# Second mixer of a two-layer recurrent block: score tile, row tile and items slot by slot on TensorE, exits of items per slot on ScalarE and VectorE

## The chip, the cores and the metric

The kernel runs on one core of one Trainium2 chip. The metric is the device time of one execution in microseconds (us). Three runs of the kernel before took 1249.71, 1252.53 and 1256.12 us; the median is 1252.53 us.

## The reference

Two layers over 2048 tokens of width 128. Only the attention of the second layer (the "second mixer") matters here. With 16 heads of size 64:

```
q, k, v = jnp.einsum('bsx,xAnh->Abnsh', input, w)
q = q + q_bias[:, None, :]
a = jnp.einsum('bnqh,bnkh->bnqk', q, k) * h ** (-0.5)
emb = jnp.einsum('sf,fnh->nsh', sins, positional * FREQS ** (-0.5))
pos_scores = jnp.einsum('bnqh,nvh->bnqv', q, emb) * h ** (-0.5)
a = a + relative_causal(pos_scores)
a = jax.nn.softmax(jnp.where(mask, a, NEG_INF), axis=-1)
o = jnp.einsum('bnqk,bnkh->bqnh', a, v).reshape(b, s, n * h)
out = o @ (out_kernel * (fan_in * fan_out) ** (-0.25)) + out_bias
```

`mask` is causal. The positional part is folded into the key and query rows (64 rows of the head, 32 of positions), so that one product of 96 rows gives `a`. The maximum of each row has to be known before the exponentials are taken; it goes into the product as a 97th row.

## The kernel before

The program before the second mixer (the first layer, its experts, the norms) is untouched and takes the first 433 us. `attention1` then walks over 8 pairs of heads (`PAIRS`). Each pair has 80 slots (`SLOTS`), 40 per head. A slot n of a pair has up to four pieces of work on TensorE:

- `score_tile(p, n)` (L1742 to L1744, three matmuls into `S[n % 2]`): scores of 128 keys (block j) against up to 512 queries (chunk c), transposed. Over a head, chunk c has 4(c+1) blocks; the last four of a chunk are diagonal tiles of 512, 384, 256 and 128 columns. ScalarE takes the exponential (`exps`, L1952) into `prob`; GpSimd splits off the low part (`plow`, L1484). Since there are two `S` buffers, `score_tile` n waits for the exponential of slot n - 2 (`s_exp`).
- `row_tile(p, n)` (L1732, one matmul into `A[n % 2]`): scores the other way round, for the row maxima of a later stretch. VectorE reduces them (`row_max`, L2051 or L2054); `row_tile` n waits for the maximum of slot n - 2 (`s_max`). The last pair has none in its last 24 slots.
- `slot_items(p, n)`: what the planner (`plan_items`) has put into that slot, at most one item: "pos", "q" or "k" (three matmuls of 512 columns, L1700 to L1702) or "v" (twelve of 128 columns, L1708 to L1710) of the next pair, "maxima" (L1713), "turn" (four transposes, L1717) and "project" (eight matmuls, L1723). Items write alternately into two buffers `M`. An item waits until the item two before it has been read out of its buffer (`s_free`). The reading out is called its exit here: "q", "k" and "v" are copied on ScalarE first (L1879, L1881, L1886) and then on VectorE (L2012, L2015, L2018), which waits for ScalarE's copy; "pos" and "project" leave by VectorE alone (L2003, L2008), "maxima" and "turn" by ScalarE alone (L1891, L1893).
- `value_tile` for slot n - 6 (`DRAIN`; L1754 to L1757, into `O`), which waits for GpSimd's `plow`.

Each engine's program is written out by hand, and each engine takes its instructions in that order. TensorE goes in steps of two slots: for slots n and n+1 it issues the score tiles of both, then row tile and items of n, row tile and items of n+1, then the two value tiles. ScalarE does the exponential of every slot, the item exits only after an odd slot (those of the two slots together), and then, at slots 8, 12, 20, 32, 48, 52, 60 and 72, `scaled` (four activations, L1966), which divides a finished chunk of `O` by its sums. VectorE does the row maximum of every slot, the item exits after an odd slot, `join_pos` at odd slots from 11 to 33, and `inverted` (L2131), for which `scaled` waits. In a pair other than the last these items stand in even slots: pos in 8, 14 and 16, turn in 10, 54, 62 and 74, q in 18, 22, 26 and 30, k in 20, 24, 28 and 32, v in 42 and 48, project in 58. The others (pos in 11, v in 55 and 63, maxima, project in 13, 65 and 77) stand in odd ones. The last pair has only turns, projects and maxima.

Of the kernel before, what the change touches and what calls it, by code (L numbers as in the profile page):

```python
# [27 lines left out]
PAIRS = HEADS // 2  # L28
# [39 lines left out]
ALL = PAIRS * SLOTS  # L68
# [26 lines left out]
def plan_items(last):  # L95

    items = {n: [] for n in range(SLOTS)}
    items[SCALE + 1].append(("turn", -1, 3))
    items[SCALE + 4].append(("project", -1, 3))
    for n, a in enumerate(A_SLOTS):  # L100
        if last and a[0] == 2:
            continue
        for c in range(NC):
            if a[1] == a_end(c) - 1 and n + 2 < SLOTS:
                items[n + 2].append(("maxima", a[0], c))
    items[1].append(("maxima", 0, 2))

    def put(n, item):

        while items[n]:  # L110
            n += 1
        items[n].append(item)
        return n

    if not last:
        n = DRAIN + 1
        for kind, c in [("pos", c) for c in range(NC)] + [(kind, c) for c in range(NC) for kind in ("q", "k")]:
            n = put(n + 1, (kind, 1, c)) + 1
        assert n <= NB - 4
    for c in range(NC - 1):  # L120
        n = put(NB + sum(TPC * (k + 1) for k in range(c + 1)) + SCALE + 1, ("turn", 0, c))
        put(n + 3, ("project", 0, c))
    if not last:
        n = NB + 2
        for c in range(NC):
            n = put(n, ("v", 1, c)) + 6
        assert n <= V_SLOT + 4
    return items
# [18 lines left out]
def ahead(p):  # L147

    return isinstance(p, int) and p == -1
# [1185 lines left out]
def attention1(nc, dram, keep, out_dram):  # L1335
# [12 lines left out]
    with ExitStack() as ctx:  # L1348
# [88 lines left out]
        plan = {}  # L1437
        for last in (False, True):
            items, k = plan_items(last), 0
# [21 lines left out]
        def count(tok, p):  # L1461

            n, b, before = tok
            return n + 1 + PER * p, b, before + (PER // 2) * p
# [221 lines left out]
        def _(pe):  # L1686
# [162 lines left out]
            for n in range(0, ALL + DRAIN, 2):  # L1849
                two = (n, n + 1)  # L1850
                for k in two:
                    if k < ALL:
                        score_tile(*divmod(k, SLOTS))
                for k in two:
                    if k < ALL:
                        row_tile(*divmod(k, SLOTS))
                        slot_items(*divmod(k, SLOTS))
                for k in two:
                    if k >= DRAIN:
                        value_tile(*divmod(k - DRAIN, SLOTS))  # L1860
# [6 lines left out]
        def _(act):  # L1867
            def item(kind, rel, c, tok, p, highs):
                it = max(p, 0) if isinstance(p, int) else p
                done, b, _ = count(tok, it)  # L1870
                a0, a1 = c * CW, (c + 1) * CW
                if kind in ("pos", "project"):
                    return
                act.wait_ge(s_item, done)
                if kind in ("q", "k"):
                    if not ahead(p) and kind == "q":
                        act.wait_ge(s_move[c], 2 * MOVES * (p + 1))
                    if kind == "q":
                        act.activation(stage[QHI][:, a0:a1], M[b][:], ACT.Identity, bias=bq[:, p + 1:p + 2]).then_inc(s_high, 1)  # L1879
                    else:  # L1880
                        act.activation(stage[KHI][:, a0:a1], M[b][:], ACT.Copy).then_inc(s_high, 1)  # L1881
                elif kind == "v":
                    if not ahead(p) and c == 0:
                        for h in (0, 1):
                            act.wait_ge(s_mv[h], 16 * (p + 1))
                    act.activation(stage_v[:, TPC * c:TPC * (c + 1), :, 0:HS],  # L1886
                                   M[b][:].rearrange("p (n h d) -> p n h d", n=TPC, h=2), ACT.Copy).then_inc(s_high, 1)
                elif kind == "maxima":
                    if rel > 0:
                        act.wait_ge(s_mrow[c], 16 * (2 * p + rel))  # L1890
                    act.activation(mrow[:, c, :], M[b][0:TPC, 0:P], ACT.Copy, scale=1.0 / M_UNIT).then_inc(s_free[b], 1)  # L1891
                elif kind == "turn":
                    act.activation(oT[:], M[b][:], ACT.Copy).then_inc(s_free[b], 1)  # L1893
# [77 lines left out]
            for n in range(ALL + SCALE):  # L1971
                if n < ALL:
                    exps(*divmod(n, SLOTS))
                    p, at = divmod(n, SLOTS)
                    if at % 2:
                        for (kind, rel, c, tok) in plan[p == PAIRS - 1][at - 1] + plan[p == PAIRS - 1][at]:
                            item(kind, rel, c, tok, p, 0)
                if n == ALL:
                    act.wait_ge(s_gate, NC)
                    for c in range(NC):  # L1980
                        at = gate[:, TPC * c:TPC * (c + 1), :]
                        act.activation(at, at, ACT.Silu).then_inc(s_silu, 1)
                if n >= SCALE:
                    scaled(*divmod(n - SCALE, SLOTS))
            kind, rel, c, tok = fin_items[0]
# [5 lines left out]
        def _(dve):  # L1991
            def item(kind, rel, c, tok, p, high):

                it = max(p, 0) if isinstance(p, int) else p
                done, b, _ = count(tok, it)
                a0, a1 = c * CW, (c + 1) * CW
                if kind in ("maxima", "turn"):
                    return
                dve.wait_ge(s_item, done)
                if kind == "pos":  # L2000
                    if not ahead(p):
                        dve.wait_ge(s_plow, NC * p + c + 1)
                    ins = dve.scalar_tensor_tensor(turned[:, c, :], M[b][:], bpos[:, p + 1:p + 2], angle[:, a0:a1], ALU.add, ALU.mult)  # L2003
                elif kind == "project":
                    if p == 0 and rel < 0:
                        dve.wait_ge(s_bias, 16)
                    s = acc[:, TPC * c:TPC * (c + 1), :]
                    ins = dve.tensor_tensor(s, M[b][:].rearrange("p (n d) -> p n d", d=D), s, ALU.add)  # L2008
                else:
                    dve.wait_ge(s_high, HIGHS * (p + 1) + high + 1)  # L2010
                    if kind == "q":
                        ins = dve.scalar_tensor_tensor(stage[QLO][:, a0:a1], M[b][:], bq[:, p + 1:p + 2], stage[QHI][:, a0:a1],  # L2012
                                                       ALU.add, ALU.subtract)
                    elif kind == "k":
                        ins = dve.tensor_tensor(stage[KLO][:, a0:a1], M[b][:], stage[KHI][:, a0:a1], ALU.subtract)  # L2015
                    elif kind == "v":
                        t = slice(TPC * c, TPC * (c + 1))
                        ins = dve.tensor_tensor(stage_v[:, t, :, HS + 1:VW], M[b][:].rearrange("p (n h d) -> p n h d", n=TPC, h=2),  # L2018
                                                stage_v[:, t, :, 0:HS], ALU.subtract)
                ins.then_inc(s_free[b], 1)  # L2020
# [103 lines left out]
            high = highs[0]  # L2124
# [8 lines left out]
            for n in range(ALL + DRAIN + 2):  # L2133
                if n < ALL:
                    p, at = divmod(n, SLOTS)
                    last = p == PAIRS - 1
                    rel, a = A_SLOTS[at]
                    if not (last and rel == 2):
                        row_max(rel % 2, a, PRO_A + at, p, 2 * p + rel)
                    high = high if at else 0  # L2140
                    if at % 2:
                        for (kind, rel, c, tok) in plan[last][at - 1] + plan[last][at]:
                            item(kind, rel, c, tok, p, high)
                            high += kind in ("q", "k", "v")
                    if at >= JOIN_SLOT and (at - JOIN_SLOT) % 2 == 0 and (at - JOIN_SLOT) // 2 < len(JOINS) and not last:
                        join_pos(*JOINS[(at - JOIN_SLOT) // 2], p)
                if n >= DRAIN + 2:
                    inverted(*divmod(n - DRAIN - 2, SLOTS))
            for c in range(NC):
                s = acc[:, TPC * c:TPC * (c + 1), :].rearrange("p n d -> p (n d)")  # L2150
                if c == NC - 1:

                    tok = fin_items[1][3]
                    dve.wait_ge(s_item, tok[0] + 1)
                    dve.tensor_tensor(s, M[tok[1]][:], s, ALU.add).then_inc(s_free[tok[1]], 1)
                else:
                    tok = next(x[3] for n in range(SLOTS) for x in plan[True][n] if x[:3] == ("project", 0, c))
                    tok = (tok[0], tok[1], count(tok, PAIRS - 1)[2])
# [148 lines left out]
```

## Time and profile before

| what | us |
|---|---|
| profiled execution, its own time | 1252.04 |
| span of its trace | 1250.0 |
| median of three runs | 1252.53 |
| PE busy (matmul) | 1168.7 (93%) |
| POOL busy | 813.2 (65%) |
| DVE busy | 803.7 (64%) |
| ACT busy | 673.5 (54%) |

PE is TensorE's matmuls, PEld its weight loads, DVE is VectorE, ACT ScalarE, POOL GpSimd. The profiled execution's own time is 2.0 us longer than its span. A matmul's row shows its start and a length that includes its way through the array, so the rows of successive matmuls overlap; what a matmul costs its successor is read from start to start.

### The profile page before, as it was taken

How to read it: one execution, taken by the hardware profiler on the slowest of the kernel's cores; microseconds unless marked ns; L12 is line 12 of the kernel's file. 1: busy time of each engine (PE TensorE's matmuls, PEld its weight loads, DVE VectorE, ACT ScalarE, POOL GpSimd, SP SyncE). 2: the span in 40 equal slices, each digit the busy share in tenths (PEclk: the TensorE clock that was granted, in tenths of full speed). 3: DMA queues.
4: the chain of work that ended last, by engine and by line, in shares of the span. 5: the costliest groups of instructions: out<-in, count | busy, mean ns of one | idle time of the engine just before them, and what ended most of it. 6: DMA issues, size and time to landing. Idle time of an engine off the chain costs nothing.

```text
span 1250.0 us, 31158 instructions
## 1 busy us (share of the span) xinstructions
PE 1168.7 (93%) x11813; PEld 759.7 (61%) x11820; DVE 803.7 (64%) x2017; ACT 673.5 (54%) x1375; POOL 813.2 (65%) x1097
## 2 busy tenths in 40 slices
PE   4899679999996999999999999999999999999997
PEld 2354455567772656666665666666666666566665
DVE  3787355752576687577668668757767766865552
ACT  2543142235533556656656656656665665665665
POOL 0777300031434488787787888878778778788886
PEclk9998768999996999999999999999999999999999
DMA  8200200001303322031030230213203113022001
GB/s 320 107 1 1 76 1 1 1 22 56 100 11 77 81 60 44 19 78 28 18 86 10 44 75 21 45 24 72 44 19 74 21 30 85 11 44 62 18 2 35
DMA packets 74752, 60.09 MB, mean 48 GB/s; under 512 B 38950, under 2 KB 69162, under 8 KB 73516
## 3 DMA queue, kind: packets, MB, share of 16 engines
q1 hardware_dynamic: 73580, 56.02, 18.1%
q0 software_dynamic: 1024, 2.09, 0.5%
q8 instruction: 94, 1.54, 0.5%
q14 instruction: 54, 0.44, 0.1%
HBM read 19.70 MB, written 4.72 MB: 20 GB/s over the span
## 4 chain that ended last, share of the span: by engine, by line
PE 63%; ACT 3%; DVE 2%; issue 1%; DMA 0%; DVEq 0%; ACTq 0%
PE S L1742 9%; PE S L1743 9%; PE A L1732 9%; PE S L1744 9%; PE O L1756 5%; PE O L1757 5%; PE O L1754 5%; PE M L1723 2%; PE M L1700 2%; PE M L1701 2%; PE M L1702 2%; ACT prob L1952 1%; ACT otok L1966 1%; PE M L1717 1%; PE M L1708 1%
## 5 line engine op out<-in xcount | busy, mean ns | idle before, releaser
L1484 POOL TENSOR_TENSOR plow<-prob 128x512 f16<-128x512 f32 (+3 forms) x640 | 577.2, 915 | 108.8 <-ACT prob L1952 86.3
L1952 ACT ACTIVATE prob<-S,keep_sigma 128x512 f32<-128x512 f32 (+3 forms) x640 | 384.6, 625 | 270.2 <-PE S L1744 269.7
L2054 DVE CUSTOM_DVE_ANT_0 junk<-A,mask_rows,part 128x512 bf16<-128x512 f32 (+3 forms) x384 | 249.7, 650 | 105.7 <-PE A L1732 67.8
L1754 PE MATMUL O<-V,prob 128*128 128x65 f16 x2176 | 232.6, 193 | 0.2 <-POOL plow L1484 0.2
L1756 PE MATMUL O<-V,prob 128*128 128x64 f16 x2176 | 232.5, 195 | 0.0
L1757 PE MATMUL O<-V,plow 128*128 128x65 f16 x2176 | 231.6, 192 | 0.0
L1742 PE MATMUL S<-rows 97*128 97x512 f16 (+3 forms) x640 | 222.9, 348 | 4.4 <-ACT prob L1952 3.0
L1743 PE MATMUL S<-rows 96*128 96x512 f16 (+3 forms) x640 | 222.3, 347 | 0.0
L1744 PE MATMUL S<-rows 96*128 96x512 f16 (+3 forms) x640 | 219.0, 345 | 0.0
L1754 PEld LDWEIGHTS O<-V,prob 128*128 128x128 bf16 x2176 | 203.3, 97 | 21.1 <-POOL plow L1484 0.3
L1756 PEld LDWEIGHTS O<-V,prob 128*128 128x128 bf16 x2176 | 202.2, 97 | 19.3
L1757 PEld LDWEIGHTS O<-V,plow 128*128 128x128 f16 x2176 | 201.9, 99 | 0.0
L1732 PE MATMUL A<-rows 96*128 96x512 f16 (+3 forms) x640 | 193.6, 347 | 1.5 <-DVE part L2054 1.2
L2051 DVE TENSOR_REDUCE part<-A 128x1 f32<-128x512 f32 x192 | 132.2, 689 | 91.9 <-PE A L1732 91.0
L1473 POOL TENSOR_SCALAR_AFFINE_SELECT prob<-prob 128x128 f32<-128x128 f32 x256 | 80.7, 315 | 31.3 <-ACT prob L1952 31.0
L1732 PEld LDWEIGHTS A<-rows 96*128 96x128 f16 x640 | 61.2, 96 | 62.4 <-DVE part L2054 8.8
L1744 PEld LDWEIGHTS S<-rows 96*128 96x128 f16 x640 | 62.6, 98 | 59.2
L766 POOL DMA_INDIRECT xe_rows<-xn_tok,slot x16 | 15.8, 988 | 119.9 <-DVE slot L1157 115.4
L1015 ACT ACTIVATE hid<-EH,b 128x512 f32<-128x512 f32 x64 | 43.9, 687 | 88.5 <-PE EH L867 88.5
L1742 PEld LDWEIGHTS S<-rows 97*128 97x128 f16 x640 | 61.6, 96 | 46.1 <-ACT prob L1952 15.8
L1743 PEld LDWEIGHTS S<-rows 96*128 96x128 f16 x640 | 62.9, 98 | 28.6
L867 PE MATMUL EH<-keep_xT,w 128*128 128x512 f32 x128 | 65.9, 622 | 0.4 <-ACT hid L1015 0.4
(352 smaller groups left out, 1870.1 us busy)
## 6 DMA issues: line engine op xcount, KB each, us to landing
rows<-stage_rows SPq DMA_DIRECT2D x64, 256.0 KB, 3.4
V<-stage_v SPq DMA_DIRECT2D x16, 516.0 KB, 4.6
W<-in_W SPq DMA_DIRECT2D x2, 2048.0 KB
shifted<-turned SPq DMA_DIRECT2D x32, 128.0 KB, 2.3
rows<-stage_pos SPq DMA_DIRECT2D x64, 64.0 KB, 3.2
w<-in_w SPq DMA_DIRECT2D x2, 1024.0 KB
xe_rows<-zero SPq DMA_DIRECT2D x1, 1280.0 KB, 9.1
ye_rows<-xe SPq DMA_DIRECT2D x5, 256.0 KB, 3.0
```

What stands on the lines that cost most here:

```text
L1473: pool.affine_select(at, at, pattern=[[1, P]], compare_op=ALU.is_ge, fill=0.0, base=0, channel_multiplier=-1).then_inc(s_cut, 1)
L1484: pool.tensor_tensor(plow[:, k % PB, 0:w], full, full.bitcast(BF16).rearrange("p (q e) -> p q e", e=2)[:, :, 1], ALU.subtract).then_inc(s_ ...
L1732: pe.matmul(out[:, 0:w], heads[h][QHI][0:RH, i * P:(i + 1) * P], heads[h][KHI][0:RH, cc * CW:cc * CW + w], start=True, stop=True).then_inc ...
L1742: pe.matmul(out[:, 0:w], kh[0:KR, k0:k1], qh[0:KR, q0:q1], start=True, stop=False, skip_group_check=True)
L1743: pe.matmul(out[:, 0:w], kl[0:RH, k0:k1], qh[0:RH, q0:q1], start=False, stop=False, skip_group_check=True)
L1744: pe.matmul(out[:, 0:w], kh[0:RH, k0:k1], ql[0:RH, q0:q1], start=False, stop=True, skip_group_check=True).then_inc(s_st, 1)
L1754: pe.matmul(both, high[:, cs, 1], vh[h][:, j, 0:HS + 1], start=(j == 0 and s == 0), stop=False, skip_group_check=True)
L1756: pe.matmul(part, high[:, cs, 1], vh[h][:, j, HS + 1:VW], start=False, stop=False, skip_group_check=True)
L1757: ins = pe.matmul(both, plow[:, n % PB, cs], vh[h][:, j, 0:HS + 1], start=False, stop=j == TPC * c + s, skip_group_check=True)
L1952: act.activation(prob[:, k % PB, 0:w], S[k % 2][:, 0:w], ACT.Exp, scale=sigma[:, 2 * p + h:2 * p + h + 1]).then_inc(s_exp, 1)
L2051: dve.tensor_reduce(out, A[g % 2][:, 0:w], AX_X, ALU.max, negate=True).then_inc(s_max, 1)
L2054: dve.tensor_tensor_reduce(junk[:, g % 2, 0:w], A[g % 2][:, 0:w], add, -1.0, before, ALU.add, ALU.min, out).then_inc(s_max, 1)
```

## The change

On TensorE the loop over two slots no longer issues both score tiles first: score tile, row tile and items of slot n come together, then those of slot n+1, then the two value tiles. On ScalarE and VectorE the exits of an item now stand right after the exponential (the row maximum) of the item's own slot, in even slots too. No instruction is added or taken away.

```
                 for k in two:
                     if k < ALL:
                         score_tile(*divmod(k, SLOTS))
-                for k in two:
-                    if k < ALL:
                         row_tile(*divmod(k, SLOTS))
                         slot_items(*divmod(k, SLOTS))
...
@@ scalar @@
                     exps(*divmod(n, SLOTS))
                     p, at = divmod(n, SLOTS)
-                    if at % 2:
-                        for (kind, rel, c, tok) in plan[p == PAIRS - 1][at - 1] + plan[p == PAIRS - 1][at]:
-                            item(kind, rel, c, tok, p, 0)
+                    for (kind, rel, c, tok) in plan[p == PAIRS - 1][at]:
+                        item(kind, rel, c, tok, p, 0)
...
@@ vector @@
                     high = high if at else 0
-                    if at % 2:
-                        for (kind, rel, c, tok) in plan[last][at - 1] + plan[last][at]:
-                            item(kind, rel, c, tok, p, high)
-                            high += kind in ("q", "k", "v")
+                    for (kind, rel, c, tok) in plan[last][at]:
+                        item(kind, rel, c, tok, p, high)
+                        high += kind in ("q", "k", "v")
```

TensorE in slots 20 and 21 of a pair, before. Slot 20 has a k item (L1700 to L1702), slot 21 the maxima (L1713):

```order
L1742 MATMUL S<-rows 128x512
L1743 MATMUL S<-rows 128x512
L1744 MATMUL S<-rows 128x512
L1742 MATMUL S<-rows 128x384
L1743 MATMUL S<-rows 128x384
L1744 MATMUL S<-rows 128x384
L1732 MATMUL A<-rows 128x512
L1700 MATMUL M<-xh,keep_pair_w 128x512
L1701 MATMUL M<-xl,keep_pair_w 128x512
L1702 MATMUL M<-xh,keep_pair_w 128x512
L1732 MATMUL A<-rows 128x128
L1713 MATMUL M<-keep_ident,negm 4x128
```

And the same two slots of the change:

```order
L1742 MATMUL S<-rows 128x512
L1743 MATMUL S<-rows 128x512
L1744 MATMUL S<-rows 128x512
L1732 MATMUL A<-rows 128x512
L1700 MATMUL M<-xh,keep_pair_w 128x512
L1701 MATMUL M<-xl,keep_pair_w 128x512
L1702 MATMUL M<-xh,keep_pair_w 128x512
L1742 MATMUL S<-rows 128x384
L1743 MATMUL S<-rows 128x384
L1744 MATMUL S<-rows 128x384
L1732 MATMUL A<-rows 128x128
L1713 MATMUL M<-keep_ident,negm 4x128
```

The score tile of the odd slot has moved behind the row tile and the item of the even slot; the rest stands where it stood.

ScalarE from slot 44 to slot 51 of a pair, before (the lines of ScalarE are two lower in the change; `scaled` is L1966 before and L1964 in the change):

```order
L1952 ACTIVATE prob<-S,keep_sigma 128x512 x5
L1966 ACTIVATE otok<-O,rsum 128x64 x4
L1952 ACTIVATE prob<-S,keep_sigma 128x384
L1886 ACTIVATE stage_v<-M 128x8x64
L1952 ACTIVATE prob<-S,keep_sigma 128x256
L1952 ACTIVATE prob<-S,keep_sigma 128x128
```

And of the change:

```order
L1950 ACTIVATE prob<-S,keep_sigma 128x512 x5
L1884 ACTIVATE stage_v<-M 128x8x64
L1964 ACTIVATE otok<-O,rsum 128x64 x4
L1950 ACTIVATE prob<-S,keep_sigma 128x384
L1950 ACTIVATE prob<-S,keep_sigma 128x256
L1950 ACTIVATE prob<-S,keep_sigma 128x128
```

The exit of slot 48's v item has moved ahead of the `scaled` of slot 48 and of the exponential of slot 49.

VectorE from slot 20 to slot 22 of a pair, before (TENSOR_REDUCE and ISA are row maxima, L2015 is the exit of the k item in slot 20, L2035 a `join_pos`):

```order
L2051 TENSOR_REDUCE part<-A 128x1
L2054 ISA junk,negm<-A,mask_rows,part 128x128
L2054 ISA negm 128x1
L2015 TENSOR_TENSOR stage_rows<-M,stage_rows 128x512
L2035 TENSOR_TENSOR stage_pos<-shifted,stage_pos 64x512
L2051 TENSOR_REDUCE part<-A 128x1
```

And of the change (L2012 there is the k item's exit):

```order
L2048 TENSOR_REDUCE part<-A 128x1
L2012 TENSOR_TENSOR stage_rows<-M,stage_rows 128x512
L2051 ISA junk,negm<-A,mask_rows,part 128x128
L2051 ISA negm 128x1
L2032 TENSOR_TENSOR stage_pos<-shifted,stage_pos 64x512
L2048 TENSOR_REDUCE part<-A 128x1
```

The k item's exit now stands ahead of the row maximum of slot 21.

## Rows read from the trace of the kernel before

**Rows 1.** The page's list of engines: busy us, share of the span, instructions.
```profile
PE 1168.7 (93%) x11813; PEld 759.7 (61%) x11820; DVE 803.7 (64%) x2017; ACT 673.5 (54%) x1375; POOL 813.2 (65%) x1097
```

**Rows 2.** Windows over the second, third and last pair: length, busy us, PEclk, DMA.
```profile
535.60:638.40 102.80, 101.58 (x1277) 66.78 (x1275) 71.80 (x176) 64.22 (x136) 83.41 (x121) 1.00 0.21 43
638.40:740.40 102.00, 101.50 (x1281) 66.91 (x1278) 71.98 (x178) 64.30 (x136) 83.42 (x121) 1.00 0.21 43
1148.60:1237.30 88.70, 86.86 (x1164) 58.08 (x1160) 41.13 (x112) 56.22 (x122) 78.72 (x111) 1.00 0.10 23
```

**Rows 3.** Waits in 436 to 1240 us: us in total, times, longest.
```profile
PEld S L1742 <- ACT prob L1952: 15.0, 39, 1.2
PEld A L1732 <- DVE part L2054: 7.2, 32, 0.6
PEld M L1700 <- DVE stage_rows L2015: 4.9, 7, 0.7
```

**Rows 4.** Timeline of PE, third pair, slots 22 and 23: start us, us.
```profile
667.35 0.38 PE L1732 MATMUL A<-rows 96*128 96x512 f16 x1
668.09 0.39 PE L1700 MATMUL M<-xh,keep_pair_w 128*128 128x512 f16 x1 [0.37 <-DVE stage_rows L2015]
```

**Rows 5.** Timeline of ACT, third pair, slots 20 to 22.
```profile
665.37 0.92 ACT L1966 ACTIVATE otok<-O,rsum 128x64 f32<-128x64 f32 x4
666.15 0.61 ACT L1952 ACTIVATE prob<-S,keep_sigma 128x384 f32<-128x384 f32 x1
666.62 0.63 ACT L1881 ACTIVATE stage_rows<-M 128x512 f16<-128x512 f32 x1
```

**Rows 6.** Timeline of DVE, third pair, the exit of slot 20's item.
```profile
667.35 0.69 DVE L2015 TENSOR_TENSOR stage_rows<-M,stage_rows 128x512 f16<-128x512 f32 x1 [0.63 <-ACT stage_rows L1881]
```

**Rows 7.** Timeline of PE, third pair, slots 62 and 63.
```profile
717.47 0.27 PE L1744 MATMUL S<-rows 96*128 96x256 f16 x1
717.87 0.23 PE L1742 MATMUL S<-rows 97*128 97x128 f16 x1
```

**Rows 8.** Timeline of PE, second pair, slots 14 and 15.
```profile
552.59 0.38 PE L1743 MATMUL S<-rows 96*128 96x512 f16 x1
552.81 0.38 PE L1744 MATMUL S<-rows 96*128 96x512 f16 x1
553.91 0.39 PE L1742 MATMUL S<-rows 97*128 97x512 f16 x1 [0.72 <-ACT prob L1952]
```

**Rows 9.** Timeline of PE, third pair, slots 48 to 50.
```profile
700.11 0.38 PE L1744 MATMUL S<-rows 96*128 96x512 f16 x1
...
700.82 0.38 PE L1732 MATMUL A<-rows 96*128 96x512 f16 x1
...
701.70 0.38 PE L1732 MATMUL A<-rows 96*128 96x512 f16 x1
...
702.20 0.27 PE L1742 MATMUL S<-rows 97*128 97x256 f16 x1
```

**Rows 10.** Timeline of ACT, third pair, slots 48 and 49.
```profile
700.53 0.69 ACT L1952 ACTIVATE prob<-S,keep_sigma 128x512 f32<-128x512 f32 x1 [0.94 <-PE S L1744]
701.11 0.92 ACT L1966 ACTIVATE otok<-O,rsum 128x64 f32<-128x64 f32 x4
701.89 0.61 ACT L1952 ACTIVATE prob<-S,keep_sigma 128x384 f32<-128x384 f32 x1
702.36 0.64 ACT L1886 ACTIVATE stage_v<-M 128x512 f16<-128x512 f32 x1
```

**Rows 11.** Timeline of PE, last pair, slots 10 and 11.
```profile
1158.94 0.27 PE L1744 MATMUL S<-rows 96*128 96x256 f16 x1
1159.75 0.23 PE L1742 MATMUL S<-rows 97*128 97x128 f16 x1 [0.54 <-ACT prob L1952]
```

**Rows 12.** Timeline of third pair: ACT in slot 33, PE in slot 35.
```profile
683.67 0.71 ACT L1952 ACTIVATE prob<-S,keep_sigma 128x512 f32<-128x512 f32 x1
...
685.12 0.38 PE L1742 MATMUL S<-rows 97*128 97x512 f16 x1
```

## The prediction

> **What bounds the kernel now.** I read the page's list of engines first [rows 1]: TensorE is busy 93% of the span. An average says little, so I took windows of one pair each [rows 2]: in the third pair TensorE is busy 101.50 of 102.00 us, GpSimd 83.4, VectorE 72, ScalarE 64. The third to seventh pair repeat this within 0.1 us; the second takes 102.80, and the last, with fewer items, 88.7. So TensorE is the bound of every pair, and the change does not touch how much it has to do. All that can change is how long TensorE stands still. The busy number hides that, because rows of matmuls overlap. I read it from start to start instead: where nothing waits, a 512-column matmul costs its successor 0.22 us [rows 8], so 384, 256 and 128 columns cost 0.16, 0.11 and 0.06.
>
> The view of waits [rows 3] names three kinds of stall in the pairs: a score tile waits for an exponential (39 times), a row tile for a row maximum (32), an item for VectorE's exit of a k item (7, once a pair but the last). These are idle times of the weight load, which runs ahead. The item's stall shows how much of it is lost: the weight load idles 0.7, while the matmul starts 0.74 after its predecessor instead of 0.22, so 0.52 are lost [rows 3, 4] and 0.18 are hidden. Taking 0.2 off each wait leaves 7.2 (S), 0.8 (A) and 3.5 (M): about 11.5 us. I then followed the starts through all eight pairs and got 12.3 us, which also holds a few short waits that the view puts elsewhere. By place:
>
> - each of the pairs 2 to 6 (counted from 0): 0.52 ahead of slot 22's item [rows 4]; 0.29 ahead of slot 63's score tile, 0.40 from start to start instead of 0.11 [rows 7]; 0.1 at slot 3's row tile; 0.1 in four small ones at slots 10, 11 and 51. Together 1.0, so 5.1 for five pairs.
> - pair 1: the same and 0.88 at slot 15, 1.10 instead of 0.22 [rows 8]: 1.9.
> - pair 0: slot 15 again, 0.52 and 0.29, and 0.8 in its first slots: 2.4.
> - the last pair: 0.70 each at slots 11 [rows 11], 51 and 63, 0.3 each at slots 23 and 75, and 0.2 in two row tiles: 2.9.
>
> 12.3 us is thus all that any order of the same work can win here: a ceiling of 1.0%.
>
> **The change part by part.** *Score tile of the odd slot behind row tile and item of the even one.* The two value tiles, and with them the next step, start where they started. Score tile n+1 waits for the exponential of n-1. It is now asked for later by the row tile (0.22) and the item (k, q, pos 0.65; v 0.67; turn 0.45; project 0.9). Where the exponential is late because ScalarE was busy, this is pure cover: slot 63's 0.29 has a row tile and a turn ahead of it (0.67) and goes; slot 15's 0.88 has a row tile and a pos (0.87) and goes, and slot 14's step is also helped as the pos exit of slot 8 leaves VectorE earlier. In the last pair slot 11 keeps 0.70 - 0.67 = 0.03, slot 23 (row tile alone) 0.07, slot 51 (row tile alone) 0.70 - 0.22 = 0.48, slot 63 (turn alone, no row tile) 0.22, slot 75 nothing: 0.8 of 2.9 stay.
>
> *Row tiles.* The even row tile comes up to 0.65 earlier, its maximum too, so VectorE no longer gets two row tiles at once and the odd maximum is ready about 0.6 earlier. The 0.1 at slot 3 goes, and most of pair 0's (0.1 stays).
>
> *Exits of even slots.* The k item of slot 20 is now finished 0.65 earlier, and ScalarE takes it ahead of `scaled` and of the exponential of slot 21. In the third pair its matmuls would start at 664.80 and end by 665.6; ScalarE's copy runs to 666.3, VectorE's to about 667.05. It ended at 668.04 before [rows 6]. Slot 22's item is ready to start at 667.4. So the 0.52 goes.
>
> The removed sum: 12.3 - 0.8 - 0.1 = 11.4 us.
>
> *What is late next.* ScalarE takes its instructions in order, and now an exit can stand ahead of an exponential of the odd slot. The odd score tile is later by the item's own length, so mostly nothing is lost. But where `scaled` stands in the same even slot, exit and `scaled` add up. That is so in slots 20, 32 and 48. I work slot 48 out in the third pair. ScalarE starts an exponential 0.04 after the end shown of its matmul (700.11 + 0.38 to 700.53) [rows 9, 10]. The row tile of 48 now starts at 700.33, the v item at 700.54; its twelve matmuls take 0.67 (701.03 to 701.70) [rows 9], so the last is over at about 701.39. ScalarE is free of the exponential from 701.11 [rows 10], waits to 701.43, copies (0.48 to its successor, as 701.89 to 702.36 and 666.15 to 666.62 show for operations of this length [rows 5, 10]), does `scaled` (0.78, 701.11 to 701.89) and starts the exponential of slot 49 at 702.69, to end at 703.30 instead of 702.50. Score tile 51 waits for it. It is asked for after score tile 50 (702.20, 0.33) and a row tile (0.22), at 702.75, as slot 50 has no item. With 0.06 from end to start it begins at 703.36: **0.61 us lost where 0.03 was, in each of seven pairs, 4.3 us.** The last pair has no v.
>
> The same in slot 32 moves the exponential of slot 33 from 683.67 to 684.45, its end to 685.14; score tile 35 stood at 685.12 [rows 12] and is asked for 0.22 later, at 685.34. It just holds, with 0.14 to spare. In slot 20 the exponential of 21 ends at about 667.5 instead of 666.76 [rows 5], and score tile 23, behind a row tile and a q item, is asked for at 668.04: 0.5 to spare. The other eleven moved exits on ScalarE have no `scaled` ahead of an odd exponential, and score tiles that had 1.4 us or more.
>
> *VectorE.* In slots 18 to 33 it has per step two maxima (0.75 each), an exit (0.67) and a join (0.7), about 3.0 us, against TensorE's 3.1. Its exit now waits for ScalarE's copy in the middle of the step and not at its end. That makes it late once, by about 1 us; being late, it finds the copy ready in the next step and the wait disappears. Row tiles had some 1.9 us in hand there, so I cost it at nothing. If this cover were gone it would be the rival below.
>
> **The sum.** Bounds for the new waits: nothing (if ScalarE's chain at slot 48 were 0.6 shorter), and 0.3 more per chain, which adds 0.3 at slot 51 and 0.16 at slot 35, 3.2 us in seven pairs. I take the 4.3 worked out, since each part of it has a row. 11.4 - 4.3 = 7.1 us gained. The tail after the last score tile keeps its order and moves as a whole. Against the profiled execution's own time: 1252.04 - 7.1 = 1244.9. It lay 0.5 under the median of the three runs, so **1245.4 us** for a median.
>
> In the rows an activation gives way to the next 0.11 before its end (0.69 long, 0.58 to the next) [rows 10]. The Trainium skill ("ScalarE: Activation LUTs", What ACT_TABLE_LOAD costs) says that back-to-back activations overlap by about 93 ns. By its figure the six handovers of the chain at slot 48 would be 0.1 us longer altogether, as an estimate, and the gain 6.4 us; the sum goes by the rows.
>
> The granted clock reads 1.00, the 2.4 GHz level, in every pair, the second with its stall of 0.88 and the last with three of 0.7 among them [rows 2, 8, 11]. So a new stall of 0.61 should not bring it down. The Trainium skill ("Perfetto Trace Analysis", Matmul Optimizations) asks for matmuls back to back in batches because the engine scales with its use. By that rule broken-up score tiles could cost clock, and each us at the lower level would add up to one more; the trace shows no fall at such gaps.
>
> **The rivals.**
> - *No new stall at slot 51*: the exponential of 49 comes in time, because the exit or `scaled` is cheaper side by side than in the chain above. Then the gain is 11.4: 1241.1. For it: ScalarE is busy only 64 of 102 us. Against it: the four steps have no slack between them. 0.12.
> - *More of the same stall*: the chains are about 0.3 longer, slot 35 stalls too, slot 51 for 0.9, or the order leaves some of the old stalls: gain 1.5 to 5, some 1248.6. For it: slot 35's margin is 0.14. 0.26.
> - *Nothing moves*: two buffers give the same distance from a tile to its reader in either order, and the late exponentials are late by as much as they are asked for later. 1252. Against it: slot 63's exponential is held by `scaled`, not by its score tile. 0.04.
> - *Slower: VectorE falls behind.* If its wait for ScalarE's copy (about 0.7 in each step of slots 18 to 33) did not vanish, a step would take it 3.7 instead of 3.1. After the 1.9 in hand, eight such steps would hold TensorE for 8 x 0.6 - 1.9 = 2.9 us a pair, 20 in seven: 13 slower, 1265. It decides from about 1 us lost per pair over the forecast's. Against it: 72 of 102 us busy. 0.04.
> - *The forecast*, 1243 to 1247.5: 0.54.
>
> **How the numbers follow.** The range reaches from rival one (1241.1, a little under it for the runs' scatter) to rival two's poorer half: 1240.5 to 1250.5, with the slower case, the unmoved one and the edges left out, 2 in 10. A measurement of this kernel tells about 0.5% (6.3 us) from no change, so faster means under 1246.2. The forecast lies 0.8 us beyond that line: of its 0.54 I count 0.41 as faster, with rival one 0.53. Same: 0.13 + 0.26 + 0.04 = 0.43. Slower: 0.04.
>
> **What would show it.** Right: a pair takes 101.5 to 101.7 in the windows, including the second; PE's wait for the k exit at L1700 gone; 7 new waits of L1742 for the exponential at slot 51 with 0.6 lost; in ScalarE's timeline the copy of v directly ahead of `scaled`; in the last pair stalls of about 0.5 and 0.2 at slots 51 and 63. Wrong: more than one stall of L1742 per pair, waits of L1732 for VectorE in slots 20 to 36, or none at slot 51.

## The result and the profile after

| | before | after |
|---|---|---|
| median of 8 runs each, us | 1250.93 (1248.29 to 1256.12) | 1240.25 (1238.52 to 1243.62) |
| profiled execution, its own time | 1252.04 | 1239.3 |
| span | 1250.0 | 1237.3 |

The ratio is 0.9915, with the interval 0.9894 to 0.9936: faster by 10.7 us, under 1% but clear of the noise. The prediction said 7.1 less, 1245.4, and a range down to 1240.5; the median lies 0.25 below that end.

The page's list of engines, after (it answers to [rows 1]):

```profile
PE 1161.3 (94%) x11820; PEld 760.1 (61%) x11820; DVE 811.4 (66%) x2017; ACT 681.7 (55%) x1375; POOL 823.0 (67%) x1097
```

Windows over the first, second, third and last pair, after: length, busy us, PEclk, DMA (the last three answer to [rows 2]):

```profile
426.90:527.50 100.60, 100.01 (x1223) 65.61 (x1224) 74.06 (x178) 65.73 (x133) 85.42 (x119) 1.00 0.20 46
527.50:629.00 101.50, 101.05 (x1280) 67.34 (x1277) 73.11 (x176) 65.35 (x136) 85.05 (x121) 1.00 0.21 44
629.00:730.60 101.60, 101.15 (x1283) 67.44 (x1280) 73.28 (x176) 65.34 (x136) 85.16 (x121) 1.00 0.21 44
1136.90:1223.10 86.20, 85.75 (x1146) 57.69 (x1143) 41.55 (x110) 56.39 (x120) 78.08 (x110) 1.00 0.11 24
```

From the start of one pair's first score tile to the next, after stands against before: pair 0 100.59 and 102.14, pair 1 101.57 and 102.95, each of pairs 2 to 6 101.57 and 102.05, the last (to its last score tile) 86.17 and 88.06. That is 1.55 + 1.38 + 5 x 0.48 + 1.89 = **7.2 us, where 7.1 were forecast**. The other 5.5 of the 12.7 by which the spans differ lie outside the pairs: 6.4 before the mixer begins, less 0.9 in the tail behind the last score tile. The first score tile, before and then after:

```profile
433.32 0.39 PE L1742 MATMUL S<-rows 97*128 97x512 f16 x1 [0.18 <-ACT kvs L1924]
```
```profile
426.88 0.39 PE L1742 MATMUL S<-rows 97*128 97x512 f16 x1 [0.18 <-ACT kvs L1922]
```

It starts 6.4 us earlier after code in which nothing was changed. The tail took 8.01 us before and 8.88 after; its granted clock reads 0.77 before and 0.67 after.

The waits of the weight load in 429 to 1227 us, after: us in total, times, longest (they answer to [rows 3]):

```profile
PEld S L1742 <- ACT prob L1950: 8.8, 18, 0.8
PEld M L1717 <- issue: 0.7, 2, 0.4
PEld A L1732 <- DVE part L2051: 0.4, 1, 0.4
PEld O L1754 <- POOL plow L1484: 0.3, 1, 0.3
```

The wait for the k exit is gone, and the 32 waits of row tiles for row maxima are one. The waits for an exponential fell from 39 to 18, with the 7 new ones at slot 51 among them. The two waits of a turn (L1717) are new; they stand in the last pair.

TensorE in the third pair, after: slots 22 and 23 (answers to [rows 4]), then 50 and 51:

```profile
657.60 0.38 PE L1732 MATMUL A<-rows 96*128 96x512 f16 x1
657.82 0.38 PE L1700 MATMUL M<-xh,keep_pair_w 128*128 128x512 f16 x1
...
658.47 0.22 PE L1742 MATMUL S<-rows 97*128 97x128 f16 x1
...
692.30 0.27 PE L1744 MATMUL S<-rows 96*128 96x256 f16 x1
692.41 0.38 PE L1732 MATMUL A<-rows 96*128 96x512 f16 x1
693.24 0.23 PE L1742 MATMUL S<-rows 97*128 97x128 f16 x1 [0.45 <-ACT prob L1950]
```

The item of slot 22 starts 0.22 behind its row tile: nothing is lost. The k exit it needs ended at 657.46, by VectorE's timeline (answers to [rows 6]):

```profile
656.77 0.69 DVE L2012 TENSOR_TENSOR stage_rows<-M,stage_rows 128x512 f16<-128x512 f32 x1 [0.42 <-PE M L1713]
```

Score tile 51 starts 0.83 behind its row tile instead of 0.22: 0.61 lost, the number of the forecast, and so in each of the seven pairs. ScalarE's timeline shows the chain that makes it late (answers to [rows 10]):

```profile
690.41 0.69 ACT L1950 ACTIVATE prob<-S,keep_sigma 128x512 f32<-128x512 f32 x1 [0.72 <-PE S L1744]
691.29 0.61 ACT L1884 ACTIVATE stage_v<-M 128x512 f16<-128x512 f32 x1 [0.20 <-PE M L1710]
691.79 0.92 ACT L1964 ACTIVATE otok<-O,rsum 128x64 f32<-128x64 f32 x4
```

The exponential of slot 49 followed at 692.57. From start to start, exponential to v copy took 0.88 (forecast 0.90), copy to `scaled` 0.50 (0.48), `scaled` to exponential 0.78 (0.78).

### The profile page after: what moved, and what is told of

It reads as the page before. It is cut to its first block, busy times and chain, and to the rows that moved or that the text cites. A ratio compares the mean times of both kernels' runs of the same rounds, so it can differ in the third digit from the quotient of the medians.

```text
span 1237.3 us, 31165 instructions
## 1 busy us (share of the span) xinstructions
PE 1161.3 (94%) x11820; PEld 760.1 (61%) x11820; DVE 811.4 (66%) x2017; ACT 681.7 (55%) x1375; POOL 823.0 (67%) x1097
## 4 chain that ended last, share of the span: by engine, by line
PE 66%; ACT 2%; DVE 1%; issue 1%; DVEq 0%
PE S L1742 10%; PE S L1743 9%; PE S L1744 9%; PE A L1732 9%; PE O L1756 5%; PE O L1757 5%; PE O L1754 5%; PE M L1723 2%; PE M L1700 2%; PE M L1702 2%; PE M L1701 2%; PE M L1717 1%; PE M L1710 1%; PE M L1708 1%; PE M L1709 1%
## 5 line engine op out<-in xcount | busy, mean ns | idle before, releaser
L1484 POOL TENSOR_TENSOR plow<-prob 128x512 f16<-128x512 f32 (+3 forms) x640 | 588.4, 930 | 94.4 <-ACT prob L1950 70.6
L1950 ACT ACTIVATE prob<-S,keep_sigma 128x512 f32<-128x512 f32 (+3 forms) x640 | 396.1, 626 | 264.6 <-PE S L1744 261.6
L1732 PE MATMUL A<-rows 96*128 96x512 f16 (+3 forms) x640 | 221.1, 346 | 1.3 <-DVE part L2051 1.0
```

Source lines behind the costliest of these rows:

```text
L1484: pool.tensor_tensor(plow[:, k % PB, 0:w], full, full.bitcast(BF16).rearrange("p (q e) -> p q e", e=2)[:, :, 1], ALU.subtract).then_inc(s_ ...
L1732: pe.matmul(out[:, 0:w], heads[h][QHI][0:RH, i * P:(i + 1) * P], heads[h][KHI][0:RH, cc * CW:cc * CW + w], start=True, stop=True).then_inc ...
L1950: act.activation(prob[:, k % PB, 0:w], S[k % 2][:, 0:w], ACT.Exp, scale=sigma[:, 2 * p + h:2 * p + h + 1]).then_inc(s_exp, 1)
```

## The experiments

Three theories about the miss. **A:** the mechanism gives its 7 us, and the rest is scatter of the 430 us ahead of the mixer, that any kernel may get. **B:** the mixer of before is slower in most runs than in the profiled one. **C:** the change itself makes the stretch ahead faster. Then there are the steps of the forecast: which part brings the gain, and what each stall costs. Twelve kernels ran in three sets, each on one chip of its own beside the kernel before: set X (e1 to e4, before 1263.85 us), set Y (e5 to e8, before 1250.29) and set Z (e9 to e12, before 1263.63). "Mixer" is the time from the start of the first score tile to the start of the last matmul: 811.37 before, 805.08 after. The ratios are those on record, taken from all runs of both kernels, and not quotients of the two medians.

### The same kernels again

e1 and e12 are copies of before, e2, e7 and e11 of the change, with no edit.

> The kernel before once more, nothing changed. The profiled pair showed 12.7 us less span, of which 6.4 us lay in the first 433 us, ahead of the second mixer. Theory A (those 6.4 us are scatter of the stretch ahead, in which matmuls run at one or the other granted clock): time within 0.3% of the kernel before; ahead of the first score tile anything from 427 to 434 us; mixer from first score tile to last matmul 811.4 us, with the same stalls at the same slots. Theory B (the mixer before is slower in other executions, e.g. at slot 15, than in the profiled one): mixer over 813 us. Theory C (the stretch ahead is always slower in the kernel before): 433 us again.

> The changed kernel once more, nothing changed. Theory A: ratio to the kernel before between 0.991 and 0.997, mixer 805.1 us, the stretch ahead anywhere from 427 to 434 us. Theory B: mixer 805.1 us and ratio again 0.9915. Theory C: the stretch ahead 427 us again, ratio 0.9915.

> The changed kernel a third time. Theory A (the part of the gain beyond the mixer's 6.3 to 7.7 us is scatter of the stretch ahead): ratio nearer to 0.9945 than to 0.9915, mixer 805 us. Theory C (the stretch ahead is always 3 to 4 us shorter in the changed kernel): ratio 0.9915 again.

> The changed kernel a fourth time, for the size of the gain. Theory A: ratio between 0.991 and 0.997 again, mixer 804 to 805 us; all four sets together nearer to 0.994, which the mixers give (7.4 us less), than to 0.9915.

> The kernel before a third time, for its mixer and the stretch ahead. Theory A: ratio 1.000, mixer 811 to 813 us, first score tile anywhere in a range of some 7 us on one chip.

| run | set | median us | ratio to before | first score tile at | mixer | clock 160 to 200 us |
|---|---|---|---|---|---|---|
| e1, before | X | 1265.69 | 0.9999 (0.9977 to 1.002) | 446.51 | 812.65 | 0.69 |
| e12, before | Z | 1265.33 | 1.0012 (0.9994 to 1.003) | 443.46 | 812.23 | 0.79 |
| e2, change | X | 1254.36 | 0.9919 (0.9893 to 0.9946) | 445.35 | 804.93 | 0.77 |
| e7, change | Y | 1243.44 | 0.9948 (0.9927 to 0.9968) | 428.23 | 803.84 | 0.78 |
| e11, change | Z | 1257.78 | 0.9952 (0.9936 to 0.9968) | 449.14 | 803.82 | 0.69 |

The mixer repeats itself: 811.4, 812.7, 812.2 for before, 805.1, 804.9, 803.8, 803.8 for the change, 7.7 between the means. Most of the rest of the scatter is the tail: from the first to the last score tile the change takes 796.2 in all four traces, before 803.4, 804.2 and 803.4. So theory B is out. The stretch ahead does not repeat itself. In set Z the change had the later start of the two (449.14 against 443.46) and in the result the earlier one, which speaks against theory C. In these two pairs the later start has the lower granted clock from 160 to 200 us; before and after in the result, then e12 and e11:

```profile
160.00:200.00 40.00, 33.36 (x136) 21.79 (x136) 18.39 (x77) 16.58 (x25) 0.00 (x0) 0.68 0.00 1
```
```profile
160.00:200.00 40.00, 33.01 (x148) 19.64 (x147) 21.66 (x76) 17.33 (x25) 0.00 (x0) 0.79 0.00 1
```
```profile
160.00:200.00 40.00, 33.28 (x150) 19.96 (x152) 21.81 (x76) 17.11 (x25) 0.00 (x0) 0.79 0.00 1
```
```profile
160.00:200.00 40.00, 33.59 (x134) 21.40 (x134) 18.34 (x63) 16.33 (x24) 0.00 (x0) 0.69 0.00 1
```

TensorE is as long busy (33 us), but with 136 matmuls instead of 148. In all fourteen profiled executions the clock there is either 0.68 to 0.70 or 0.77 to 0.79, with either order of the mixer. Of those that start their mixer below 434 us, the first kind start it at 433.3, 431.4 and 433.2 and the second at 426.9, 428.2 and 426.4. In set Z it is the same (446.8 and 449.1 against 443.5 and 442.8). In set X it is not: 446.5 and 444.6 with the lower clock, 445.3 and 445.5 with the higher. This one window is therefore a sign of the scatter and not the whole of it.

The other executions have no trace, but for those of the three sets the record has the mean granted clock of the whole span. It varies as the time does: in set Y the 17 times of before run from 1245.35 us at 0.972 to 1253.73 at 0.964. A straight line through the runs of a set, with one slope for all its kernels, gives 0.9 to 1.1 us more for each 0.001 of clock less. Compared at equal clock, the change is 9.0 us faster in set X (plus or minus 1.7), 7.2 in Y (1.1) and 7.2 in Z (1.2), as estimates from these fits. The mean clock covers the tail too, so this does not say where the time was lost. With the mixers and the starts it supports theory A: the change is worth 7 to 8 us, and much of the scatter of whole times moves with the granted clock. The four ratios weighted by their intervals give 0.994, 7.8 us, and the mixers 7.7. They differ by somewhat more than their intervals allow, and set X stays on the high side at equal clock; why is open. The start at 427 to 434 us that was expected of e1 and e2 was missed: all of set X starts its mixer later.

### e3: TensorE's new order alone

Before, with this edit; all exits stay after odd slots.

```
                 for k in two:
                     if k < ALL:
                         score_tile(*divmod(k, SLOTS))
-                for k in two:
-                    if k < ALL:
                         row_tile(*divmod(k, SLOTS))
                         slot_items(*divmod(k, SLOTS))
```

> TensorE's new order alone, exits after odd slots as before. My theory: the stall at slot 51 is not there (the v copy stands behind the exponential of 49 again), but slot 22's item waits for the late k exit, 0.68 us a pair; slot 63, 15, 3 lose nothing. Sum: 6.3 us less in the mixer, as much as the whole change. Rival (the early exits bring the gain): less than 2 us gained.

Median 1271.74, ratio 1.0054 (1.0033 to 1.0076); mixer 819.28. I had expected 6.3 less than before, and it is 7.9 more (811.37): my expectation fell, and the rival stood. TensorE in the third pair at slot 22, and VectorE's exit that it waits for:

```profile
682.60 0.38 PE L1732 MATMUL A<-rows 96*128 96x512 f16 x1
683.91 0.39 PE L1700 MATMUL M<-xh,keep_pair_w 128*128 128x512 f16 x1 [0.93 <-DVE stage_rows L2013]
```
```profile
683.16 0.69 DVE L2013 TENSOR_TENSOR stage_rows<-M,stage_rows 128x512 f16<-128x512 f32 x1 [0.92 <-ACT stage_rows L1879]
```

1.31 instead of 0.22: 1.09 lost where before lost 0.52, 0.92 more at slot 30 and 0.15 at slot 18. The item is asked for earlier, while the copy on ScalarE still stands behind the exponential of the odd slot, which is now later. Without the exits per slot the new order loses more than it wins; they are worth 819.3 - 805.1 = 14.2 us with it.

### e5: the exits per slot alone

The change, with TensorE's two loops of before:

```
                         score_tile(*divmod(k, SLOTS))
+                for k in two:
+                    if k < ALL:
                         row_tile(*divmod(k, SLOTS))
```

> The exits per slot alone, TensorE in the old order. My theory (an exit ahead of the odd exponential is paid for only where the odd score tile is later by the item too): slots 23, 35 and 51 stall 0.9, 0.75 and 1.3 us, slot 63 keeps 0.3: 2.4 us a pair more than before in seven pairs, mixer 828 us, ratio 1.013. Rival (the early exits are good by themselves, since the order after which they come late cost 14 us): mixer under 811.

Median 1266.12, ratio 1.0128 (1.0102 to 1.0154); mixer 827.36, as expected (828). TensorE at slots 50 and 51, third pair:

```profile
705.23 0.27 PE L1744 MATMUL S<-rows 96*128 96x256 f16 x1
706.65 0.23 PE L1742 MATMUL S<-rows 97*128 97x128 f16 x1 [1.15 <-ACT prob L1952]
```

ScalarE, with the copy of v ahead of the exponential of 49:

```profile
704.71 0.60 ACT L1886 ACTIVATE stage_v<-M 128x512 f16<-128x512 f32 x1 [0.69 <-PE M L1710]
```

An exit ahead of the odd exponential stands waiting for an item that TensorE issues behind the odd score tile; so score tile 51 loses 1.31. Slots 23 and 35 lose 0.90 and 0.74 in the same way and slot 63 keeps 0.29, all as expected; 0.17 at slot 31 was not. Each half alone costs 8 and 16 us, both together win 6 to 8: TensorE's order and the place of the exits are one decision.

### e6 and e9: one engine's exits late

The change; e6 has the exits of both slots after the odd one on VectorE, e9 on ScalarE (shown; e6 is the same in VectorE's loop):

```
-                    for (kind, rel, c, tok) in plan[p == PAIRS - 1][at]:
-                        item(kind, rel, c, tok, p, 0)
+                    if at % 2:
+                        for (kind, rel, c, tok) in plan[p == PAIRS - 1][at - 1] + plan[p == PAIRS - 1][at]:
+                            item(kind, rel, c, tok, p, 0)
```

> The change with VectorE's exits after odd slots as before, ScalarE's per slot. My theory (ScalarE's place carries it, VectorE's is worth little): mixer 805 to 807 us, the stall at slot 51 stays 0.61, slot 22's item waits 0 to 0.1. Rival (VectorE's place matters as much): stalls at slots 18, 22 and 30 as in TensorE's order alone, mixer over 812.

> The change with ScalarE's exits after odd slots as before, VectorE's per slot: the fourth corner of the square (TensorE's new order with both late: mixer 819.3; VectorE late: 810.3; none late: 805.1). My theory: ScalarE's place is worth more than VectorE's, and VectorE now stands still at an even item until ScalarE has done the odd exponential, so that its odd row maxima come late too: mixer 820 us or more, no stall at slot 51, stalls of items or row tiles in slots 18 to 33. Rival (the places add up one by one, 9 us for ScalarE's): mixer 813 to 815.

e6: median 1250.26, ratio 0.9997 (0.998 to 1.0014), mixer 810.33. It was expected at 805 to 807, by the rival over 812, and lies between. Slot 22's item loses nothing and slot 51 keeps its 0.61, as expected, but slots 18 and 30, which the rival named, lose 0.15 and 0.52 in every pair but the last (the first loses some 1.0 more near slots 14 to 18). In the third pair slot 30's item starts 0.58 behind a row tile of 128 columns, whose share is 0.06, so 0.52 are lost:

```profile
678.23 0.22 PE L1732 MATMUL A<-rows 96*128 96x128 f16 x1
678.81 0.39 PE L1700 MATMUL M<-xh,keep_pair_w 128*128 128x512 f16 x1 [0.36 <-DVE stage_rows L2012]
```

e9: median 1300.49, ratio 1.0292 (1.0262 to 1.0321), mixer 846.33, as expected ("820 us or more"). VectorE, then TensorE at slot 22, third pair:

```profile
682.55 0.75 DVE L2010 SCALAR_TENSOR_TENSOR stage_rows<-M,keep_bq,stage_rows 128x512 f16<-128x512 f32 x1 [2.10 <-ACT stage_rows L1877]
```
```profile
685.24 0.38 PE L1732 MATMUL A<-rows 96*128 96x512 f16 x1
687.10 0.39 PE L1700 MATMUL M<-xh,keep_pair_w 128*128 128x512 f16 x1 [1.49 <-DVE stage_rows L2013]
```

The weight load's waits in e9:

```profile
PEld A L1732 <- DVE part L2052: 17.3, 21, 1.6
PEld M L1700 <- DVE stage_rows L2013: 16.7, 14, 1.9
PEld A L1732 <- DVE negm L2052: 15.7, 29, 1.4
```

VectorE comes to the exit in the even slot, ScalarE makes the copy only after the odd one, and VectorE stands 2.1 us with the row maximum of the odd slot behind it. Slot 22's item loses 1.65 by that. It is not alone: slots 30, 35 and 37 lose 0.95, 1.70 and 0.27 and the row tile of slot 51 loses 1.60, 6.2 us in each pair but the last. That row tile was not in the expectation, which named slots 18 to 33. With TensorE's new order the mixer takes:

| | ScalarE's exits per slot | ScalarE's exits late |
|---|---|---|
| VectorE's exits per slot | 805.1 (the change) | 846.3 (e9) |
| VectorE's exits late | 810.3 (e6) | 819.3 (e3) |

ScalarE's place is worth 9 us when VectorE's is late and 41 when it is not. Of e9's 846.3, 1.3 us come from the clock and not from the order (see the point on the clock below).

### e4 and e8: no v item in slot 48

The change, with the v item of slot 48 in slot 49, so that no `scaled` follows its copy ahead of an odd exponential:

```
-            n = put(n, ("v", 1, c)) + 6
+            n = put(n + (n == 48), ("v", 1, c)) + 6
```

> The changed kernel with the planner putting the v item of slot 48 into slot 49, where its exit stands behind the exponential of 49 as before. My theory: the stall of 0.61 us at slot 51 goes in seven pairs and no other comes: mixer 800.8 us, 4.3 us less than the change, 10.6 less than before. Rival (another wait is right behind, TensorE only stalls later): less than 1 us gained over the change.

> The variant with the v item in slot 49 once more, beside the changed kernel on the same chip. Theory A: mixer 800.8 us, median 4 us under that of the changed kernel within the scatter of 2. Theory C (what the mixer gains the stretch ahead loses): the same median again.

Mixer 800.82 and 800.58 (expected 800.8). TensorE at slots 50 and 51, third pair, e4:

```profile
708.93 0.27 PE L1744 MATMUL S<-rows 96*128 96x256 f16 x1
709.04 0.38 PE L1732 MATMUL A<-rows 96*128 96x512 f16 x1
709.26 0.22 PE L1742 MATMUL S<-rows 97*128 97x128 f16 x1
```

Score tile 51 follows its row tile by 0.22; the 0.61 is gone in seven pairs. Medians: 1254.36, ratio 0.9923 (0.9897 to 0.9949), beside e2's 1254.36 and 0.9919; and 1237.81, ratio 0.9904 (0.9876 to 0.9932), beside e7's 1243.44 and 0.9948. From the first to the last score tile it takes 792.2 in both, 4.0 less than the change. That showed in one set of times and not in the other. The mean clock on record accounts for a part: e4's runs had 0.964 on average and e2's 0.966, and at equal clock e4 is 2.4 us faster than e2 (plus or minus 2.1) and e8 4.1 faster than e7 (1.4), by the fits above. So 4.0 agrees with both sets.

### e10: `scaled` ahead of the exit in slot 48

The change, with `scaled` of slot 48 ahead of the item's exit on ScalarE:

```
                     p, at = divmod(n, SLOTS)
+                    if at == 48:
+                        scaled(*divmod(n - SCALE, SLOTS))
...
-                if n >= SCALE:
+                if n >= SCALE and (n % SLOTS != 48 or n >= ALL):
```

> The change with the four activations of scaled put ahead of the v exit in slot 48, on ScalarE. Nothing is shorter, only the 0.32 us that ScalarE waits for the v item are filled. My theory of the chain at slot 48: the stall at slot 51 is 0.29 instead of 0.61, mixer 802.8. Rival (the stall is the v copy's length or its place, not the wait): 0.61 stays, or goes altogether.

Median 1261.22, ratio 0.9973 (0.9954 to 0.9991); mixer 807.84 instead of 802.8. The third pair at slot 51 on TensorE, and VectorE's exit of v:

```profile
713.39 0.38 PE L1732 MATMUL A<-rows 96*128 96x512 f16 x1
713.91 0.23 PE L1742 MATMUL S<-rows 97*128 97x128 f16 x1
...
714.91 0.34 PE L1732 MATMUL A<-rows 96*128 96x384 f16 x1 [0.66 <-DVE part L2053]
```
```profile
713.49 0.69 DVE L2017 TENSOR_TENSOR stage_v<-M,stage_v 128x512 f16<-128x512 f32 x1 [1.20 <-ACT stage_v L1884]
```

The score tile loses 0.30 (0.52 instead of 0.22), as expected (0.29), so half of the 0.61 is ScalarE's wait for the v item. What I had not followed is VectorE: the copy starts 1.38 behind the exponential of 48 instead of 0.88, VectorE stands 1.2 us for it with the row maximum of 49 behind, and row tile 51 waits 0.8 for that.

## Why the prediction was right, and where it missed

- **The ceiling, the old stalls.** Right. The k item's 0.52, slot 63's 0.29, slot 15's and the row tiles' are gone in pairs 1 to 6. Pair 0 won 2.2 ahead of the new stall, 2.3 forecast: 0.12 stays at the row tile of slot 3, as forecast, and 0.36 and 0.16 at the score tiles of slots 2 and 4. The loss at slot 15 is of each execution's own size: in pairs 0 and 1 it is 0.82 and 0.89 in the profiled before, 1.21 and 1.29 in e1, 1.20 and 0.52 in e12. So the ceiling of 12.3 is one execution's figure; e1's would have been some 0.9 higher.
- **The last pair.** 1.9 won, 2.1 forecast: the steps of slots 11, 23, 51 and 63 keep 0.11, 0.08, 0.49 and 0.30 (forecast 0.03, 0.07, 0.48, 0.22). Score tile 51, then the step of slot 63:

```profile
1191.35 0.38 PE L1732 MATMUL A<-rows 96*128 96x512 f16 x1
1192.05 0.23 PE L1742 MATMUL S<-rows 97*128 97x128 f16 x1 [0.32 <-ACT prob L1950]
...
1205.15 0.27 PE L1744 MATMUL S<-rows 96*128 96x256 f16 x1
1205.55 0.63 PE L1717 MATMUL M<-keep_ident,otok 128*128 128x128 f32 x4
```

  At slot 63 the size of the forecast is near by luck. Score tile 63 itself no longer stalls; 0.29 are lost ahead of the turn of slot 62, 0.40 from start to start instead of 0.11. The turn reads `otok`, so it waits for `scaled`, whose four activations ended at 1205.40:

```profile
1204.48 0.92 ACT L1964 ACTIVATE otok<-O,rsum 128x64 f32<-128x64 f32 x4
```

  Before, the stall of score tile 63 (0.67) stood ahead of the turn and hid this wait. The forecast counted the turn as cover and did not ask what the turn itself waits for.

- **The new stall.** Right, 0.61 in seven pairs; e4 and e8 take away its cause and win 3.3 to 4.3 us. Slot 35, with its margin of 0.14, lost nothing in any pair. So rivals one and two are both out. In these rows an activation still gives way 0.11 before its end (691.29 + 0.61 against 691.79). The Trainium skill ("ScalarE: Activation LUTs", What ACT_TABLE_LOAD costs) says that back-to-back activations overlap by about 93 ns; by that, as an estimate, the stall would have been 0.7, and the rows decide.
- **VectorE at nothing.** Right for the change: no wait of an item on it is left. But the cover is thin, since moving its exits by one slot (e6) costs 5.3 us. The mechanism of the slower rival is real: e9 has a stronger form of it, with VectorE standing 2.1 us for a copy where the rival had 0.7, and loses 41 us where 20 were counted. It does not start here because ScalarE's copy moves with VectorE's exit.
- **The clock.** It reads 1.00 in the mixer after too, with 0.6 lost seven times, and even in e3, third pair, with its gaps of 1.1:

```profile
653.80:757.10 103.30, 101.61 (x1282) 67.12 (x1279) 72.77 (x177) 64.50 (x136) 85.68 (x121) 1.00 0.20 43
```

  It is not so for gaps of any size and number. In e9, with 6.2 us lost in a pair, it fell once, in the seventh pair; the window, then three matmuls in it that start 0.41 to 0.43 apart instead of 0.22:

```profile
1137.60:1141.00 3.40, 3.40 (x31) 2.15 (x30) 2.40 (x5) 0.64 (x1) 1.61 (x2) 0.50 0.02 5
```
```profile
1138.85 0.62 PE L1742 MATMUL S<-rows 97*128 97x512 f16 x1
1139.26 0.63 PE L1743 MATMUL S<-rows 96*128 96x512 f16 x1
1139.69 0.63 PE L1744 MATMUL S<-rows 96*128 96x512 f16 x1
```

  Just before it TensorE had lost 0.68 at slot 35's score tile and 1.02 at its row tile, as in the six other pairs, where the clock stayed at 1.00. This pair took 108.6 us and the others of its kind 107.4. The Trainium skill ("Perfetto Trace Analysis", Matmul Optimizations) wants matmuls back to back in batches. The traces of the change show no cost of clock from its new stall; e9's agrees with the page, with 1.3 us.

**The step that failed** is the one from the sum to a median: "1252.04 - 7.1 = 1244.9. It lay 0.5 under the median of the three runs". The sum took the 433 us ahead of the mixer as fixed, and the range gave "a little under it for the runs' scatter". By [rows 2] every window that I had read was of the mixer. Two things were left out. The median of before over 8 runs is 1.6 lower than that over three, so 1250.93 - 7.1 = 1243.8 was the value of the sum. And the stretch ahead moves by up to 6 or 7 us from one execution to the next, in good part with the clock that it is granted; a median over eight still moves by some of that. So the time came out nearest to rival one (1241.1), whose mechanism was absent. The runs show in place of that step: 7.2 us between the first and last score tiles of the profiled pair, 7.8 by the times of all four sets, and a start of the mixer 6.4 us earlier in the profiled pair, which no term stood for. A range with 3 us of such scatter at both ends would have held the time. How the 10.7 of the first set divides beyond its profiled execution stays open: its other runs have no trace, and the record has no clock for those of before.

## What to carry to other kernels

Ahead of a prediction compare executions also where nothing is changed: a stretch that the profile shows at a clock below 1.00 may differ by several us between runs, and a gain of the same size needs a trace of each side, read from a fixed point in it. Where each run's mean granted clock is on record, compare the times at equal clock as well. When exits of a buffer pass through two engines in order, move the producer's order and the place of both exits together; leaving one of the three as it was cost 5 (VectorE), 22 (TensorE) or 41 us (ScalarE) here. When a piece of work is counted as cover for a wait, look at what that piece itself waits for. Look then for the place where two instructions that were apart now stand ahead of the same exponential, since moving one item by a slot (e4, e8) won back what the change had lost there.

## What was not expected of the hardware

- The granted clock in 160 to 200 us is 0.68 to 0.70 or 0.77 to 0.79 in executions of one program, and never between, in the fourteen profiled. What decides it is open.
- The sets differ ahead of the mixer: it starts at 426 to 433 us in the result and set Y, at 443 to 449 in X and Z. Each set was on one chip. In the eight traces of X and Z ScalarE waits 8.3 to 14.9 us in all, in the experts' layer between 255 and 300 us, for something that the profile calls "remote"; the six traces of the result and set Y have no such wait there. From e2:

```profile
288.59 1.27 ACT L1015 ACTIVATE hid<-EH,b 128x512 f32<-128x512 f32 x2 [9.16 <-remote]
```

  Behind these waits TensorE is 13 to 14 us later than at the same matmul in the result's execution of the change, of 18 at the first score tile. GpSimd's wait for `ye_rows` is longer there too (51.2 against 41.0 us), but it ends only at 337 us, when those 13 to 14 us are already lost. What "remote" is, and whether the chip makes the difference, no run shows.
- The tail varies with the granted clock too: the last 13 to 14 us of the span read 0.67 in the change's execution, 0.77 in before's and 0.79 in e7, with 8.88, 8.01 and 7.65 us from the last score tile to the last matmul.
